# Cross attentions of a four-layer decoder: the second half's norm, its query bank and the order in which values are kept

## The reference, cut to what matters

```python
def layernorm(x):
    return (x - mean(x)) / sqrt(var(x) + 1e-5)

# layers 1, 2 and 3: keys and values from the context
q = layernorm(x) @ Wq + bq;  k = ctx @ Wk + bk;  v = ctx @ Wv + bv
p = softmax(q @ k.T / sqrt(8))          # layer 3: masked per sequence
x = x + (p @ v) @ Wo + bo

# layer 0: queries and keys from the normed state, values from the context
q = layernorm(x) @ Wq + bq;  k = layernorm(x) @ Wk + bk;  v = ctx @ Wv + bv
o = softmax(q @ k.T + shifted_causal_mask) @ v
x = x + gelu(o @ W1 + b1) @ W2 + b2
```

## Time and profile before

| | |
|---|---|
| median of 3 runs | 1343.27 us (1342.66 to 1344.61) |
| the profiled execution's own time | 1342.8 us |
| its span, first to last instruction | 1341.0 us |
| PE busy | 1116.9 us, 83% of the span |
| DVE busy | 775.2 us, 58% |
| ACT busy | 660.2 us, 49% |
| POOL busy | 332.5 us, 25% |
| mean granted clock of PE, of full speed | 0.904 |
| X0 with its MLP begins | 131.7 us |
| X1 begins | 324.6 us |
| X2 begins | 878.0 us |
| X3 begins | 1146.1 us |

### The profile page before, as it was taken

How to read it: one execution, slowest core, us unless ns; L and a number is a source line. 1 busy time by engine, 2 the same in 40 slices (tenths; PEclk the granted TensorE clock), 3 DMA queues, 4 the chain that set the end, 5 groups by cost and what they waited for, 6 DMA issues and landing times. The chain is left out here.

```text
span 1341.0 us, 25706 instructions
## 1 busy us (share of the span) xinstructions
PE 1116.9 (83%) x9898; PEld 721.7 (54%) x9899; DVE 775.2 (58%) x1948; ACT 660.2 (49%) x1386; POOL 332.5 (25%) x320
## 2 busy tenths in 40 slices
PE   6898784598889975779869865979889988798998
PEld 4565563346666642347527634847434444475776
DVE  4565546586665478867886786546362565453111
ACT  2564343463452245777686662535656443345332
POOL 1333200023210026464564520240000034700000
PEclk9999897599899977869978995889899989899999
DMA  7000000200000000000000000080196710000000
GB/s 304 1 2 2 1 3 0 97 0 1 3 1 1 1 1 0 1 2 1 1 1 2 1 0 1 2 339 14 31 193 127 159 17 1 2 3 1 1 0 16
DMA packets 18329, 44.83 MB, mean 33 GB/s; under 512 B 4992, under 2 KB 8096, under 8 KB 17568
## 3 DMA queue, kind: packets, MB, share of 16 engines
q1 hardware_dynamic: 18208, 43.20, 11.2%
HBM read 42.41 MB, written 0.79 MB: 32 GB/s over the span
## 5 line engine op out<-in xcount | busy, mean ns | idle before, releaser
L930 ACT ACTIVATE L_xattn_pT<-banks 128x512 f32<-128x512 f32 x128 | 69.0, 598 | 87.9 <-PE banks L808 87.9
L241 POOL TENSOR_TENSOR norm_rstd<-norm_var,norm_power 128x4 f32<-128x4 f32 x24 | 24.6, 1026 | 345.9 <-DVE norm_var L234 345.8
L991 DVE TENSOR_REDUCE L_xattn_top<-banks 128x4 f32<-128x512 f32 x128 | 79.5, 684 | 36.3 <-PE banks L776 36.3
L1576 DVE TENSOR_TENSOR L_ffn_a<-L_ffn_a,L_ffn_share 128x512 f32<-128x512 f32 x64 | 39.9, 685 | 61.0 <-DMA L_ffn_share<-L_ffn_shares 60.6
L1803 ACT ACTIVATE L_ffn_aT<-banks,L_ffn_shift 128x512 f32<-128x512 f32 x64 | 43.3, 687 | 58.9 <-PE banks L1755 57.3
L1490 PE MATMUL banks<-L_ffn_a,region_a 128*128 128x512 f32 x136 | 67.5, 601 | 5.1 <-DVE L_ffn_a L1576 5.1
L1816 DVE SCALAR_TENSOR_TENSOR x<-banks,L_ffn_combine,x 128x128 f32<-128x128 f32 x64 | 18.0, 344 | 88.7 <-PE banks L1766 88.7
L1481 PE MATMUL banks<-hT,region_a 128*128 128x512 f32 x136 | 68.8, 611 | 0.0
L1766 PEld LDWEIGHTS banks<-region_b,L_ffn_aT 128*128 128x128 f32 x512 | 59.4, 192 | 6.7 <-issue 6.7
L490 ACT ACTIVATE L_attn_p<-banks,L_attn_shift 128x129 f32<-128x129 f32 x128 | 45.4, 369 | 33.0 <-DVE L_attn_shift L540 33.0
L1755 PE MATMUL banks<-hT,region_b 128*128 128x512 f32 x128 | 59.6, 609 | 0.0
(11 more groups left out here) (546 smaller groups left out, 2890.8 us busy)
## 6 DMA issues: line engine op xcount, KB each, us to landing
L_ffn_share<-L_ffn_shares SPq DMA_DIRECT2D x32, 512.0 KB, 10.8
region_b<-in_L_ffn SPq DMA_DIRECT2D x1, 6216.0 KB, 30.1
region_a<-in_L_ffn SPq DMA_DIRECT2D x1, 4416.0 KB, 13.2
region_b<-in_L_attn SPq DMA_DIRECT2D x1, 3150.5 KB, 10.5
region_a<-in_L_ffn SPq DMA_DIRECT2D x1, 3080.5 KB, 21.2
region_b<-in_L_attn SPq DMA_DIRECT2D x1, 1633.5 KB, 9.1
region_b<-in_L_xattn SPq DMA_DIRECT2D x1, 835.0 KB, 9.7
w_tables<-in_tables SPq DMA_DIRECT2D x1, 832.0 KB, 12.6
```

What stands on the lines that cost most here:

```text
L930: nc.scalar.activation(pT[:, n % 2, 4 * i:4 * i + 4, :], rows_of(flip[i][:], 4), ACT.Exp, scale=scale).then_inc(exped, 1)
L991: nc.vector.tensor_reduce(top[:, 32 * i:32 * i + 32:HD], rows_of(score[i][:], 4), X, ALU.max).then_inc(topped, 1)
L1576: nc.vector.tensor_tensor(a[:, k % AHEAD, :], a[:, k % AHEAD, :], share[:, batch % RING, j, :], ALU.mult).then_inc(weighed, 1)
```

## The change

It has five edits, all in `small_head_attention`.

1. DVE's order. In X1 and X2 the moments and the scaling of the second half come first and `keep_keys` after them. In X0 the moments stand between the second and the third mask copy, and the scaling behind the third.
2. `split` is false in X0: ACT spreads all 512 columns of the first keys, and DVE none.
3. The second half's queries go into bank 4, from which hT was kept, instead of bank 7; PE's wait for `v_kept` in `make_queries(1)` goes.
4. In X0 PE issues `make_queries(1)` and the second keys behind turn_top(0) and scores(1), instead of ahead of turn_top(0).
5. ACT's order: values of half 1 are kept behind the second queries (in X0 behind the second keys too); in X0 hT's second half is kept ahead of values 0.

```diff
-    split = Norm.is_kept(g)
+    split = Norm.is_kept(g) and shared_mask is None
...
-    hT_bank, q_bank, ... = (bank[0], bank[4]), (bank[2], bank[7]), ...
+    hT_bank, q_bank, ... = (bank[0], bank[4]), (bank[2], bank[4]), ...
...
             def make_queries(half):
                 norm.await_kept(pe, half)
-                if half == 1:
-                    pe.wait_ge(v_kept, 1)
...
             scores(0)
             norm.turn(pe, 1, hT_bank[1])
-            make_queries(1)
-            if keys_here:
-                make_more_keys()
+            if not keys_here:
+                make_queries(1)
             turn_top(0)
             for k in range(1, LAST):
                 if k < B:
                     scores(k)
+                if keys_here and k == 1:
+                    make_queries(1)
+                    make_more_keys()
...
-            keep_values(0)
-            if not keys_here:
+            if keys_here:
+                norm.keep(act, 1, hT_bank[1])
+                keep_values(0)
+            else:
+                keep_values(0)
                 keep_more_keys()
-            keep_values(1)
-            norm.keep(act, 1, hT_bank[1])
+                norm.keep(act, 1, hT_bank[1])
             keep_queries(1)
             if keys_here:
                 keep_more_keys()
+            keep_values(1)
...
             if shared_mask is not None:
-                keep_shared_mask()
+                copy_corners()
+                keep_shared_mask(0, mask_turned[:], T)
+                keep_shared_mask(1, by_query[:].rearrange("p m k -> p (m k)"), HALF)
+            norm.take_moments(dve, 0)
+            norm.take_moments(dve, 1)
+            if shared_mask is not None:
+                keep_shared_mask(2, by_key[:].rearrange("p m k -> p (m k)"), HALF)
+            norm.scale(dve, 0)
+            norm.scale(dve, 1)
             if split:
                 keep_keys()
-            norm.take_moments(dve, 0)
-            norm.take_moments(dve, 1)
-            norm.scale(dve, 0)
-            norm.scale(dve, 1)
```

More of the change, by code:

```diff
@@ L644, in small_head_attention @@
     turned_bank, out_bank = bank[4], bank[5][:, 0:D]
-    hT_bank, q_bank, k_bank, v_bank = (bank[0], bank[4]), (bank[2], bank[7]), (bank[1], bank[6]), (bank[7], bank[5])
+    hT_bank, q_bank, k_bank, v_bank = (bank[0], bank[4]), (bank[2], bank[4]), (bank[1], bank[6]), (bank[7], bank[5])
     keys_here = keys_from is g.hT
@@ L971, in _, with copy_corners, keep_shared_mask @@
         def _(dve):
-            def keep_shared_mask():
+            def copy_corners():
                 nc.vector.tensor_copy(copies[:], bc(g.ident_bf[:].rearrange("p (m q) -> p m q", m=4), 2, 4)).then_inc(copies_ready, 1)
[L974 to L977, removed]
+            def keep_shared_mask(m, out, cols):
+                dve.wait_ge(mask_made, m + 1)
+                nc.vector.tensor_copy(out, mask_banks[m][:, 0:cols]).then_inc(mask_kept, 1)
             def keep_keys():
```

## The result

| | median of the runs | runs | profiled execution | its span | mean granted clock |
|---|---|---|---|---|---|
| before, beside the runs of after | 1347.76 us | 20 (1340.93 to 1354.40) | 1342.8 | 1341.0 | 0.904 |
| after | 1339.47 us | 20 (1333.88 to 1345.72) | 1339.99 | 1338.2 | 0.905 |

After takes 0.994 of the time of before, 95% interval [0.9924, 0.9957]: 8.1 us gained (5.8 to 10.2) where 14.6 were forecast, and 1339.5 lies outside the range of 1325 to 1335. The 10.8 us by which the forecast is off are 4.5 of base (the three runs that it stood on were low: the median of before beside the runs of after is 1347.76, not 1343.27) and 6.3 to 6.5 of gain.

A forecast was written before the change was run, and what follows sets the result against it. Queue waits were taken to delay the openings, with PE the bound from 352.24 on; gains of 5.8 (X1), 5.4 (X2) and 3.4 (X0), 14.6 off 1342.8, gave 1328.2, plus 0.47 a median of 1328.7 us, range 1325 to 1335.

The forecast's parts named there:

- The 4.2 us from first to second scores in X1: X1's opening: with the norm first, second scores come at 337.1 instead of 341.27, 4.2 us sooner.
- the clock term of 1.6: X1, second to fourth scores: PE keeps the full clock, 9.3 instead of 10.97, 1.6 us; bounds 0 and 1.7.
- X2, 5.4: X2 repeats X1's gain: first to fourth scores 13.8 instead of 19.52, 5.7, less 0.3 for late code.
- held by late code or by its weight transfers: Rival in X2: late code or weight transfers hold it, so X2 brings only 2.5; 1331.6 us, chance 0.06.
- The row of 0.66: X2 at 909.50: PE stood 0.66 for nothing shown; possibly late code, bounds 0 and 1.3 lost, 0.3 taken.
- X0, 3.4: X0: flip_scores(0) comes sooner, 4.2 us less some 0.5, or 2.5 if the clock falls; middle 3.4 taken.
- The tail of ScalarE that I named as late next: X0: ScalarE keeps the values last, and flip_scores(0) waits for them; it costs X0 some 0.5.
- The keys' slack: Time by which VectorE's keys end before PE's first scores: 0.6 in X1 and 0.4 in X2.
- keys late: Rival in X1 and X2: keys beside POOL's clearing last 1.4 longer, 0.8 and 1.0 lost; 1330.5, chance 0.09.
- the rival of a held scaling: POOL's clearing holds the scaling throughout, its four instructions taking 7.65 in X1; 2.4 slower, 1345.7, chance 0.04.
- the X1 term: X1: chain of 4.2 plus clock of 1.6, 5.8 us, all reaching the stage's and the program's end.
- steady state gives it back: Rival: ACT or DVE, not PE, sets the pace further on and stages end as before; about 1343, chance 0.05.

The follow-up runs named there:

- r2_norm_first: The kernel before with only VectorE's order changed in X1 and X2, the keys moved behind the norm's scaling; median 1341.39 us, ratio to before 0.9956.
- r4_before_c: The kernel before, unchanged, the last of three further profiled executions; 1347.28 us.
- r2_loads_later: The changed kernel with L3_ffn's weights asked for two stages later, in layer 3's mixing block; median 1334.26 us, ratio to before 0.991.
- r4_after: The changed kernel, unchanged, a third profiled execution; 1338.22 us.
- r5_nf_x1: The kernel before with VectorE's keys moved behind the norm's scaling in X1 alone; median 1346.08 us, ratio to before 0.9982.
- both r5 kernels: The kernel before with VectorE's keys moved behind the scaling in X1 alone or in X2 alone; medians 1346.08 and 1344.92 us.
- r3_nf_shift: r2_norm_first with the scores products of five batches done twice in X1; median 1345.59 us, ratio to before 0.9991.
- r4_before_a: The kernel before, unchanged, the first of three further profiled executions; 1346.38 us.

## Why the prediction was wrong

*The chains: right from the first scores on.* The 4.2 us from first to second scores in X1 came out at 4.20 (8.66 to 4.46), the clock term of 1.6 at 1.68 (10.97 to 9.29 from second to fourth scores). VectorE's order carries nearly all of it (r2_norm_first). From an equal entry (r4_before_c) X1's fourth scores come 4.7 sooner and not 5.8: 0.8 goes to the keys below, and 0.4 to the clock, which the old order loses less of when X1 opens at full clock (19.20 from first to fourth scores in place of 19.63). X3 stayed, 5.25 between its first two scores as before.

*X2, 5.4: mis-sized.* The chain gave 4.7 at the fourth scores and 4.1 at the fifth (25.39 to 21.28). The fifth scores of X2, before:

```profile
911.20 1.14 PE L776 MATMUL banks<-L_xattn_ks,L_xattn_qT 32*128 32x512 f32 x8
```

The rival "held by late code or by its weight transfers" was true for 2.7 us at the fifth scores: without L3_ffn's transfer they come 18.60 behind the first, 6.8 sooner than before. The row of 0.66 was the sign, and a stand with a transfer of 6 MB beside it should have been priced at more than 0.3. The Trainium skill, "Runtime: NRT & Kernel Launch", section "Instruction fetch mechanics", has such crossings mostly hidden; that agrees with X1, where no execution has a stand, and with X2 once that transfer is gone (r2_loads_later). Beside the transfer each of the three executions of after has stands in X2, their sum 1.0 to 2.3, and the six of before have 0.2 to 1.1.

*X0, 3.4: mis-sized.* I took 3.4, between 2.5 and 4.2, though PE's wait of 2 us was in the forecast itself; the clock fell, and 2.4 came, the lower end. The tail of ScalarE that I named as late next is there, 1.31.

*The keys' slack: too large where PE comes early.* The rival "keys late" had the wrong cause, since the keys did not lengthen beside POOL's clearing (1.89). That agrees with the Trainium skill, "SBUF — State Buffer", section "SBUF: two separate sides". But the 0.6 of slack was that of an X1 which opens at the lower clock; where it opens at full clock PE is ready for its first scores 6.3 behind the opening, not 7.9. The keys end at 6.9 or 7.5, as the scaling ahead of them takes 2.12 or 2.73, and PE waits 0.72 in after and 1.32 in r4_after. In r5_nf_x1 the scaling took 4.14 and the wait was 1.06. So it is the scaling that can last longer beside POOL's clearing, as the rival of a held scaling had it, though not near that rival's 7.65.

*The step that failed* is the last of the X1 term: "Behind the fourth scores PE is the bound as before, so the 5.8 of both terms reach the stage's end and, since all engines meet there, the program's." To the stage's end they came: over the six profiled executions of before and the three of after X1 is 6.1 shorter, X2 4.8 and X0's attention 2.8, together 13.7 against my 14.6. To the program's end they did not. Of the unchanged stages the stretch behind X1 is 3.7 longer, the state space 2.7, and layer 0's attention, which no edit precedes, 4.2; the MLP and the ternary stage behind X0's attention are 1.4 shorter, the rest 0.4, and the spans differ by 4.9 on average. Without layer 0's attention it would be 9.1, near the 8.1 of the medians.

What of that belongs to the change? Layer 0's attention cannot: it took 131.2 to 137.7 over the kernels.

The state space was 67.7 to 68.0 or 70.8 to 73.3. The longer form came in five of the thirteen executions whose X0 has the old order (r4_before_c and r5_nf_x1 among them) and in six of the seven with the new one. Scatter alone could do that; but in all twenty it went with the time from X0's start to the state space: the longer form behind 121.8 or less, the shorter behind 121.9 or more. X0's edit shortens that time, so a part of X0's 2.8 may have been given back here, which would fit the 0.9 that X0 alone brought. No run tests it.

The stretch shows more. With X1's waits as before it took 489.8 to 489.9 in five of eight executions and 492.3 to 492.7 in three; with them shortened in any way 492.3 to 495.1 in all twelve, the means 490.9 and 494.1. So by these means about 3.2 of X1's gain were given back there. The 2.4 that X1 alone brought fits that, though its interval (0 to 4.9) holds the stage's whole 4.4 too. It was one of my rivals in name ("steady state gives it back"), but I looked for it within the stage, at ScalarE and VectorE, and gave it 0.05.

The sum of single gains also failed because it was taken between one execution of before, 5.0 under the later median of that kernel (1342.8 to 1347.76), and an average execution of after.

*What stays open*: why a shortened X1 goes with the lower clock in the stretch. The time at which the stretch begins does not decide it (386.31 in both r5 kernels). X1's length does not decide the whole (r3_nf_shift), but the short stretch never followed an X1 under 63.5, whichever order it had, and no run gave the new order so long an X1. And with intervals of about 5 us the runs cannot split the missing 6 between the stretch, the state space, X2 and X0.

## What to carry to other kernels

A shortened chain is worth what its stage shows only if the stages behind it keep their granted clock: compare the unchanged stages of both traces, by length and clock, before adding up gains, and take several executions of the kernel before, for one of them can lie 5 us under the kernel's median. Look beside a stand with "issue" for a large transfer and for code that lands just before the stand ends, and move the transfer: here that took 1.3 to 3.1 off X2. Slack that is measured at the lower clock shrinks when the engine enters the stage at full clock: here 0.6 of slack became a wait of 0.7 to 1.3.

## What the runs showed of the hardware

Unchanged code moved by more than single edits did. The same first eight products of layer 1's experts, before and in r5_nf_x1:

```profile
388.24 3.67 PE L1645 MATMUL banks<-hT,region_a 128*128 128x512 f32 x8 [1.32 <-PEq L78]
```

```profile
386.31 5.35 PE L1648 MATMUL banks<-hT,region_a 128*128 128x512 f32 x8 [1.32 <-PEq L78]
```

The idle time ahead of them is the same 1.32, and the length goes from 3.67 to 5.35. These products alone do not decide the stretch: in after they take 3.67 too, and it is 4.0 longer than in before. And the forms repeat to a tenth: four executions of before have the stretch at 489.83 to 489.92, with the same 1.00 in the 20 us from 140 on, and a fifth that differs there (r4_before_a) is 2.8 longer with every stage ahead within 0.1 of the first's.

VectorE's four scalings beside POOL's clearing took one of three lengths. Over X1 and X2 of the twenty profiled executions it was 2.12 eleven times, 2.7 twenty-eight times and 4.14 once, with the same instructions on both engines.
